# The third layer's first norms, turns and projections placed in the last steps of the routed pipeline, and the experts' activations in other tiles

## The reference, cut to what matters

```
x = x + gate * attention(norm(x))            # l0, with rope and a mask
x = x + gate * attention(norm(x), context)   # l0c
x = x + gate * gelu(norm(x) @ W1) @ W2       # perceptron
nx = norm(x); evidence = softmax(nx Wq k) v  # routed layer
r = sum_e softmax(router)_e * (silu(nx, evidence @ w1_e) @ w2_e)
x = x + sigmoid(silu(nx, evidence @ g1) @ g2) * (r @ out_w)
x = x + attention(norm(x), norm(context))    # l2, "the third layer"
x = x + attention(norm(x)); x = x + attention(x, context); x = x + mlp(norm(x))
```

## Time and profile before

| | us |
|---|---|
| median of 3 runs | 1228.96 (1228.44 to 1229.12) |
| the profiled execution, its own time | 1224.47 |
| its span, first to last instruction | 1222.6 |
| PE busy | 1120.1 (92%) |
| DVE busy | 778.9 (64%) |
| ACT busy | 603.7 (49%) |
| POOL busy | 595.4 (49%) |

### The profile page before, as it was taken

The page is one execution under the profiler, slowest core; times in us unless marked ns, Lnnn a source line. Parts: engine busy times, 40 slices in busy tenths (PEclk is TensorE's granted clock), DMA queues, the critical chain, the costliest instruction groups (busy, mean ns, idle before and its releaser), DMA issues.

```text
span 1222.6 us, 29544 instructions
## 1 busy us (share of the span) xinstructions
PE 1120.1 (92%) x12119; PEld 703.3 (58%) x12119; DVE 778.9 (64%) x1896; ACT 603.7 (49%) x940; POOL 595.4 (49%) x602
## 2 busy tenths in 40 slices
PE   4799999999998997999999489999999999999998
PEld 2345555666655774666666245565555566656576
DVE  5767777667674433666766557777888776677421
ACT  0044444566666534444444136566555555655663
POOL 5365556566763431111210667666575544457421
PEclk9699999999999997999999559999999999999999
DMA  4300000000000102000000000000000000000001
GB/s 166 122 3 3 11 19 11 11 19 19 14 16 20 43 27 82 11 6 6 6 7 6 16 6 7 2 2 2 2 2 2 2 2 2 2 2 2 2 27 43
DMA packets 9284, 22.94 MB, mean 19 GB/s; under 512 B 1392, under 2 KB 1648, under 8 KB 8768
## 3 DMA queue, kind: packets, MB, share of 16 engines
q1 hardware_dynamic: 9152, 21.07, 5.1%
HBM read 18.90 MB, written 2.15 MB: 17 GB/s over the span
## 4 chain that ended last, share of the span: by engine, by line
PE 76%; DVE 12%; issue 6%; POOL 3%; ACT 3%; DMA 0%; DVEq 0%; POOLq 0%; ACTq 0%
PE weighed L595 12%; PE scores L568 10%; PE row_scores L537 6%; PE scores L737 5%; PE weighed L632 4%; DVE negmax L1047 4%; PE scores L477 3%; PE scores L501 3%; PE scores L494 3%; PE row_scores L737 3%; PE scores L487 2%; PE scores L580 2%; PE scores L456 2%; PE turns L605 2%; PE row_scores L748 2%
## 5 line engine op out<-in xcount | busy, mean ns | idle before, releaser
L1047 DVE TENSOR_REDUCE negmax<-row_scores 128x8 f32<-128x616 f32 (+1 forms) x312 | 300.7, 964 | 123.8 <-PE row_scores L537 94.7
L1420 ACT ACTIVATE p<-scores 128x1024 f32<-128x1024 f32 (+1 forms) x256 | 247.7, 1018 | 191.3 <-PE scores L580 191.3
L1575 POOL TENSOR_TENSOR kblk_r<-work,pack_const 128x308 fp32r<-128x308 f32 (+1 forms) x160 | 134.0, 838 | 244.5 <-PE row_scores L537 242.8
L568 PE MATMUL scores<-qblk,work 32*77 32x512 f32 (+1 forms) x1280 | 187.8, 629 | 11.6 <-DVE hat L1003 3.6
L1565 POOL TENSOR_TENSOR qblk<-work,pack_const 128x512 f32<-128x512 f32 x160 | 166.1, 1038 | 20.8 <-PE scores L568 20.1
L595 PE MATMUL weighed<-p,v 77*32 77x128 f32 (+1 forms) x5120 | 174.2, 277 | 0.9 <-DVE hat L1003 0.9
L595 PEld LDWEIGHTS weighed<-p,v 77*32 77x32 f32 (+1 forms) x5120 | 130.9, 110 | 46.6 <-issue 43.6
L537 PE MATMUL row_scores<-kblk_r,qr 32*128 32x308 f32 (+1 forms) x624 | 138.3, 433 | 19.7 <-DVE negmax L1047 18.0
L580 PE MATMUL scores<-nblk,select 32*77 32x512 f32 (+1 forms) x640 | 139.0, 802 | 0.0
L537 PEld LDWEIGHTS row_scores<-kblk_r,qr 32*128 32x128 f32 x624 | 63.4, 190 | 106.1 <-POOL kblk_r L1575 53.0
L1420 ACT ACTIVATE p<-scores,neg_kb 77x1024 f32<-77x1024 f32 x64 | 67.6, 1105 | 38.1 <-PE scores L580 38.1
(11 more groups left out here) (272 smaller groups left out, 1985.1 us busy)
## 6 DMA issues: line engine op xcount, KB each, us to landing
shared<-gates_hbm SPq DMA_DIRECT2D x24, 256.0 KB, 3.2
shared<-in_ctx_tok SPq DMA_DIRECT2D x16, 154.0 KB
pack_w_l<-in_w_l SPq DMA_DIRECT2D x1, 2058.5 KB, 9.9
x<-in_x_tok SPq DMA_DIRECT2D x8, 256.0 KB, 6.2
out_x<-x SPq DMA_DIRECT2D x8, 256.0 KB, 2.0
layers_w<-in_w_l SPq DMA_DIRECT2D x1, 1289.0 KB, 9.1
ctxT<-in_ctxT SPq DMA_DIRECT2D x1, 1232.0 KB, 9.2
layers_w<-in_w_l SPq DMA_DIRECT2D x1, 640.0 KB, 6.9
```

Source lines behind the costliest of these rows:

```text
L568: mm = e.matmul(scores[0:nk, g, :], k_of[q % 3][at, s * nk:(s + 1) * nk], qblk[n % 2][at, :], start=layer.mask != "qk", stop=False, skip_g ...
L1047: e.tensor_reduce(negmax[q % 2][:, 2 * h:2 * h + 2, 0, s * NJ:(s + 1) * NJ], row_banks(n, h)[:, :, 0:NJ * nk].rearrange("p g (j k) -> p g ...
L1420: e.activation(p[n % 2][0:nk, 8 * h:8 * h + 8, :], scores[0:nk, 2 * h:2 * h + 2, :].rearrange("p g (j q) -> p (g j) q", j=NJ), ACT.Exp, bi ...
L1575: e.tensor_tensor(kblk_r[n % 2][:, 0:NJ * nk].rearrange("p (j k) -> p j k", j=NJ), k_of[q % 3][:, s * nk:(s + 1) * nk].unsqueeze(1).to_bro ...
```

## The change

The first four norms of the third layer (K0, Q0, K1, Q1), the first quad's two projections, and what goes with them are issued inside the routed loop's steps 6 to 9 by every engine but SP: `attention` takes a first and a last `t`, and the engines call pieces of it between the routed layer's parts. The waits between the stages stay, but ACT's now stands at t = -7 (ahead of `round_q`) and the others' at t = -6. Statistics and roots of the four norms come earlier than their slots say (`slots_of`), and so do the `normalise_x` of K0 and Q0. `hidden[0]` and `hidden[1]` change places, so that quad 7 lies in `normT` and `qblk[0]` and leaves `work` free, and `mix_in[0]` lies in `qblk[1]` and leaves `hat` free. No instruction is added or left out but waits; SP's order is the same.

```diff
--- before.py
+++ after.py
...
 NORM_AT = [{it.slot: it for it in NORMS if (it.q >= 2 * NB) == bool(phase)} for phase in range(2)]
-STATS_AT = [{(it.slot - 2 if it.family else it.slot - 3, it.family): it for it in at.values()} for at in NORM_AT]
 BEFORE = {it.index: max([-1] + [o.index for o in NORMS if o.family == it.family and o.k == it.k - 1]) for it in NORMS}
...
 A_NORMS = sum(it.q < 2 * NB for it in NORMS)
+
+
+def slots_of(it):
+
+    n, run_up = it.index - A_NORMS, 4 * PHASES[1][0] - 16
+    if 0 <= n < 4:
+        return run_up + n // 2, run_up + n // 2, (run_up + 2, run_up + 2, it.slot - 1, it.slot - 1)[n]
+    return (it.slot - 2, it.slot - 1, it.slot - 1) if it.family else (it.slot - 3, it.slot - 2, it.slot - 1)
+
+
+STATS_AT, ROOT_AT, XHAT_AT = ({} for _ in range(3))
+for it_ in NORMS:
+    for at_, slot_ in zip((STATS_AT, ROOT_AT, XHAT_AT), slots_of(it_)):
+        at_.setdefault((it_.q >= 2 * NB, slot_), []).append(it_)
...
         evT = attnT
-        hidden = [[quad(normT, 2 + k) for k in range(6)] + [work[:, 7, :]], [work[:, k, :] for k in range(7)]]
+        hidden = [[work[:, k, :] for k in range(7)], [quad(normT, 2 + k) for k in range(6)] + [qblk[0][:, :]]]
         gate_z, gate_sig = four(1, 1), [four(1, 2), four(1, 3)]
-        mix_in = [hat[:, 0:NE * D], four(1, 0)[:, 0:NE * D]]
+        mix_in = [qblk[1][:, 0:NE * D], four(1, 0)[:, 0:NE * D]]
         mix_step = pair
...
-            def attention(phase):
+            def attention(phase, first=-16, last=None):
+
                 lo, hi = PHASES[phase]
+                end = 4 * hi + TAIL if last is None else 4 * lo + last
                 jobs, quads, norm_at = range(4 * lo, 4 * hi), range(lo, hi), NORM_AT[phase]
...
-                for t in range(4 * lo - 16, 4 * hi + TAIL):
+                for t in range(4 * lo + first, end):
...
                         hidden_layer(c, 1)
+                    if i == NB + 1:
+                        attention(1, -8, -7)
                     if old:
...
                         expert_mix(m, 1)
+                    if i == NB:
+                        w.wait_ge(r_pT, NB)
+                        w.wait_ge(r_logged, NB)
+                        w.wait_ge(g_z, NB - 1)
+                        attention(1, -16, -12)
+                    if i == NB + 1:
+                        attention(1, -7, -6)
                     if last:
...
                         expert_mix(m, 3)
+                    if i == NB:
+                        attention(1, -12, -10)
                     if last:
...
                         evidence_logits(i)
+                    if i == NB:
+                        attention(1, -10, -8)
                     if last:
                         hidden_layer(c, 6)
+                        if c == NB - 1:
+                            w.wait_ge(ln_scaled, A_NORMS + 3)
                         gate_layer(c)
...
             routed()
-            attention(1)
+            attention(1, -6)
...
                     mix(m, 1)
+                if i == NB:
+                    attention(1, -14, -12)
+                if i == NB + 1:
+                    attention(1, -8, -6)
                 if last:
...
                     mix(m, 3)
+                if i == NB:
+                    attention(1, -12, -10)
                 if last:
...
                     router_max(i)
+                if i == NB:
+                    attention(1, -10, -8)
                 if last:
...
                     output_biases()
+                if i in (6, 7):
+                    attention(1, i - 22, i - 21)
             w.wait_ge(m_done, QUAD * NB)
-            attention(1)
+            attention(1, -6)
...
-                    it = norm_at.get(t + 1)
-                    if it and it.family:
-                        if t > 4 * hi:
-                            e.preload_act_table_set("natural_log_exp_and_others")
-                        root(it)
+                    roots = ROOT_AT.get((phase == 1, t), ())
+                    for it in roots:
+                        if it.family:
+                            if t > 4 * hi:
+                                e.preload_act_table_set("natural_log_exp_and_others")
+                            root(it)
                     if phase == 0 and t == 4 * hi + 10:
...
                         take_pair(t - 1)
-                    it = norm_at.get(t + 2)
-                    if it and not it.family:
-                        root(it)
+                    for it in roots:
+                        if not it.family:
+                            root(it)
                     if cl == 1 and qi + 2 in quads:
...
                     e.activation(r_le[:, :, :], r_le[:, :, :], ACT.Exp).then_inc(r_lexp, 1)
+                if i in (7, 8):
+                    attention(1, i - 23, i - 22)
                 if i + 1 < NB:
...
                     gate_sigmoid(c)
+                if i == NB:
+                    attention(1, -14, -7)
                 if i + 1 < NB:
...
             w.wait_ge(d_added, NB)
-            attention(1)
+            attention(1, -7)
...
                         shift_normed(norm_at[t - 1])
-                    if t + 1 in norm_at:
-                        normalise_x(norm_at[t + 1])
-                        if norm_at[t + 1].kind == "l3f":
-                            w.wait_ge(ln_xhat, norm_at[t + 1].index + 1)
-                            add_rows(norm_at[t + 1].c, "l3_b2", ffn_biased)
+                    for it in XHAT_AT.get((phase == 1, t), ()):
+                        normalise_x(it)
+                        if it.kind == "l3f":
+                            w.wait_ge(ln_xhat, it.index + 1)
+                            add_rows(it.c, "l3_b2", ffn_biased)
                     if cl == 1 and qi in quads and not layer_of(qi).gated:
...
                     routed_x(i + 1)
+                if i == NB:
+                    attention(1, -13, -11)
+                if i == NB + 1:
+                    attention(1, -7, -6)
                 if m >= 0:
...
                     e.tensor_tensor(xs, xs, mixed[m % 2][:, :], ALU.add).then_inc(d_added, 1)
+                if i == NB - 1:
+                    w.wait_ge(r_turned, NB)
+                    attention(1, -16, -13)
+                if i == NB:
+                    attention(1, -11, -7)
             w.wait_ge(d_added, NB)
-            attention(1)
+            attention(1, -6)
```

20 lines of the change are left out of this document (11 added, 9 removed).

## The result

| | before | changed |
|---|---|---|
| first comparison, median (range), runs | 1228.70 us (1222.81 to 1229.12), 4 | 1211.76 us (1209.74 to 1212.43), 4 |
| second comparison | 1224.19 us (1222.61 to 1229.15), 11 | 1213.98 us (1210.53 to 1217.12), 6 |
| all executions, mean (median) | 1225.9 us (1224.6), 50 | 1212.8 us (1212.3), 10 |
| profiled execution, span | 1224.47 us, 1222.6 | 1212.27 us, 1210.1 |

The ratio is 0.9873 in the first comparison, 95% interval 0.9847 to 0.9899, and 0.9899 (0.9871 to 0.9926) in the second. The change makes the kernel about 1.1% faster. The two medians differ by 17 us in the first and by 10 in the second, since the kernel before has two levels: of its 50 executions 28 lie at 1222.6 to 1225.8 (mean 1223.8) and 22 at 1227.1 to 1231.6 (mean 1228.5).

What follows compares the result with a forecast made beforehand. PE, busy 92% of the span, bounds the kernel, so time is won only where it waits or runs at low clock. Terms -12.6 and -0.5 sum to -13.1 us: 1228.96 to 1215.9, said as 1216, range 1210.5 to 1221.

Steps and rivals of the forecast that it cites:

- Steps 6 and 7: Routed steps where DVE takes statistics of K0, Q0, K1, Q1: costed at nothing, 5 us at most if cover were gone.
- Step 8: Routed step with early queries and K1 turns: new 1.1 us wait for POOL, first mix of quad 7 3.8 us later.
- Rival (a): Routed steps lose clock at PE's new wait before K1's turns, costing 1.7 us: 1217.6; chance 0.17.
- Step 9: Quad 7's mixes on DVE: 7.96 us, plus 1.9 for scaling and statistics, plus 0.3 for POOL beside them; done at 679.7.
- port term: POOL's spreading of first keys beside DVE's mixes delays one or two of eight two-SBUF-input instructions: 0.3 us taken.
- bound of 0.7: Upper limit, in us, for mix delay from POOL's key spreading, if a whole POOL instruction were waited for; sum then -12.7.
- First row scores 12.6 us sooner: Third layer's first row scores start at 683.2 instead of 695.84, after PE idles some 7.4 us.
- The ramp gives 0.5: Behind the first row scores, the second ones no longer wait for DVE's maximum: 0.5 us won, bounds 0 to 1.3.
- rival (b): Start of the third layer gives back some 2 to 4 us of the gain: 1218 to 1220; chance 0.15.
- The clock ... comes back at the same place in the program: Clock falls in the new idle time as in the old and returns at the same program point; no gain or loss.
- Rival (c): Clock returns sooner in the third layer's start: about 4 us more won, or twice that, 1208 to 1212; chance 0.10.
- Carrying 4.5 us over from the profile to the median: Median of runs lay 4.5 us above the profiled execution; the same difference was assumed after the change.

Runs made afterwards that it cites:

- combined_b: Changed kernel, reordered: K2's statistics before quad 7's mixes, Q1 scaled between second and third, rounding freed from the residual add, POOL's gate and add later; 1209.24 us.
- cast_early: Changed kernel with ACT's rounding of the first queries moved ahead of its wait for quad 7's residual add; 1211.62 us.
- fill8: Changed kernel with 8 added matmuls, results unused, in PE's idle time before the first row scores; 1209.52 us.
- tiles_only: Kernel before with only the tiles for hidden parts and mix_in changed, no instruction moved; 1225.89 us, ratio 1.0011.
- dense_fill: Changed kernel with 8 added matmuls before the first row scores and one in each of six steps up to the first exact scores; 1205.54 us, ratio 0.9822.
- fill: Changed kernel with 14 added matmuls, results unused, on PE behind quad 7's last mix; they held the row scores up by 4.5 us; 1214.78 us.

## Why the prediction came out as it did

The forecast was 1216 with 1210.5 to 1221, the measured median 1211.76: inside, 4.2 us below the value. The mechanism held, two steps about the clock didn't. The 4.2 is nearly the 4.5 us that the last step of the sum carried over.

- **Steps 6 and 7 cost nothing:** right. PE is busy all of 640 to 660, and DVE still waits 0.55 for PE before its first mix of quad 6 (654.75).
- **Step 8:** right in kind and size. No wait for the queries (0.16), 0.93 before the turns of K1 where I said 1.1, the first mix 3.47 us later counted from the gate layer (forecast 3.8). Rival (a), lost clock there, didn't come: 1.00 in 660 to 676.
- **Step 9:** DVE took 9.98 us from the first mix's start to the last one's end (forecast 7.96 + 1.9 + 0.3 = 10.2). The scaling and the statistics put 1.79 between the second and the third mix (3.36 us from one's start to the other's, 1.57 before) where I said 1.9. The port term was 0.27, one instruction, near my 0.3, though it fell on one with a single tensor input and not on one of two SBUF inputs. My bound of 0.7 held for one short spread of keys only: in `combined_b`, beside three POOL instructions of 1.04 us, the term is 1.8.
- **First row scores 12.6 us sooner:** 13.18, behind 7.43 us of idle time (7.4). The 0.6 is 0.3 in step 8, 0.2 in step 9, and roundings. That ACT's rounding ends it is shown by `cast_early`, and `fill8`'s trace names it. What the waits for the rounding and for gate and add cost is not additive, though: freeing the first one moved the first exact by 0.9 only.
- **The ramp gives 0.5:** 0.28, up to the first exact. Of rival (b) (2 to 4 us given back) the first profile shows nothing. In the second, 1.3 us are given back behind the first exact (503.60 against 502.28), by a later return of the clock.
- **"The clock ... comes back at the same place in the program":** wrong as a step. It came back 15.3 us behind the first exact in the profile of before, 8.0 and 18.3 in two of the changed kernel, and from 7.9 to 20.8 in all those profiles in which it fell there; `tiles_only`, with PE's order of before, had it at 8.6. Rival (c) had the mechanism for the first profile (2.07 us), but as luck of one execution and not as an effect of the change.
- **Carrying 4.5 us over from the profile to the median:** wrong. The profile of before fell in the lower of its two levels and the median of the runs shown in the upper (4.7 us between the means of the two), so the 4.5 was a difference of levels and not of profiled and timed executions; the changed kernel's first four runs all lay low (mean granted clock 0.960 to 0.963, where three of the next six had 0.956 and took 1215.5 to 1217.1). The term that I worked out, -13.1, is also what the means of all executions show (1225.9 to 1212.8). That it fits so exactly is luck: the clock alone set the two profiles of the changed kernel 3.3 us apart, and ten executions are few.

What stays open: why the changed kernel doesn't show two clear levels as the kernel before does (its ten executions spread from 1209.7 to 1217.1), and where the clock is lost in the upper level, in one more short fall in the routed steps or by a later return behind the ramp. Of the timed executions only the mean granted clock is on record, and no trace of the kernel before in its upper level was taken.

## What to carry to other kernels

Read a gap by the chain that fills it, and put the ends of that chain under the stage before; but then ask of each wait what stands queued behind it on the same engine: here freeing the first start alone (4.4 us) was worth little (0.9), since the next one still waited. Where PE idles a few microseconds between stages, price the low clock behind it as well as the idle time: here 5.6 to 9 us, and 14 matmuls that compute nothing, in PE's waits, bought it back. Read the mean granted clock of every execution before comparing medians. Compare profiles by distances from an instruction ahead of the change, not by absolute times, before explaining a few microseconds.

## What the runs showed of the hardware

- Filling the long idle time alone didn't keep the clock: in `fill` it fell while PE had waits of 1.05 and 1.34 us between short pieces of work, at about 692, 5 us behind the last added matmul; in `fill8` it fell at about 686, 3 us behind the last one, behind waits of 0.56 and 1.05 us. With one matmul of about 1 us more in each step (`dense_fill`) it stayed at 1.00.
- The return to full speed was found anywhere from 7.9 to 20.8 us behind the first exact in executions in which PE did the same work there; by my estimate from two profiles each microsecond of it costs about 0.35 us ((504.50 - 497.3) / 20.8).
- The mean granted clock separates the two levels of the kernel before without an exception in 46 executions: 0.954 or more at up to 1225.8 us, 0.953 or less from 1227.1 on.
- A DVE instruction with one tensor input in SBUF and a column of scalars (L1321, 128x128) took 0.56 us beside a POOL instruction instead of 0.29, and ended 0.09 us behind it (675.10 and 675.01). The Trainium skill (SBUF — State Buffer, "Who interferes with whom") has two cases for DVE, two SBUF inputs, and a two-port mode that a `tensor_scalar` can enter; the trace agrees that it can be held up, and doesn't tell which case it was.
